# Attention on one core: two pairs of heads at a time, seven banks in rotation

## What is computed

```
x_norm = layernorm(xn, ln_g, ln_b)
q, k, v = x_norm @ Wq + bq, x_norm @ Wk + bk, x_norm @ Wv + bv      # (N, 8, 64)
ws  = (q[origin] . k[destination]) * SCALE * edge_weights           # per edge and head
att = softmax of ws over the edges of one origin
values = segment_sum(att * v[destination], origin)
y   = (values @ W1 + b1) @ W2 + b2
x   = x + (xn + y) + linear_attention(xn)                           # xn = layernorm(x), the layer's input
x   = x + ffn(layernorm(x))      # digits read out of 48 columns, shifted, added back as one-hot
```

## Time and profile before

| | us |
|---|---|
| median of 3 runs | 802.64 |
| lowest and highest | 800.6 and 811.86 |
| the profiled execution | 803.23 |
| its span in the trace | 801.5 |
| TensorE busy (PE) | 736.1 |
| VectorE busy (DVE) | 563.7 |
| ScalarE busy (ACT) | 388.2 |
| GpSimd busy (POOL) | 401.3 |
| attention's first scores | at 352.72 |

### The profile page before, as it was taken

The page is one execution under the profiler, slowest core; times in us unless marked ns, Lnnn a source line. Parts: engine busy times, 40 slices in busy tenths (PEclk is TensorE's granted clock), DMA queues, the critical chain, the costliest instruction groups (busy, mean ns, idle before and its releaser), DMA issues.

```text
span 801.5 us, 13739 instructions
## 1 busy us (share of the span) xinstructions
PE 736.1 (92%) x4643; PEld 446.3 (56%) x4682; DVE 563.7 (70%) x1295; ACT 388.2 (48%) x917; POOL 401.3 (50%) x399
## 2 busy tenths in 40 slices
PE   1997798898999999979999999999999999999984
PEld 0543345544445654436666666666666876667662
DVE  4468767684223252349998998999999887788696
ACT  0411110122130223117777777878788866566561
...
PEclk9999799998999999999999999999999999999996
...
GB/s 233 196 272 328 316 301 243 241 337 293 246 183 183 178 297 295 39 5 148 175 150 173 154 170 158 164 119 213 161 202 79 138 94 123 150 97 92 93 1 128
DMA packets 69636, 143.66 MB, mean 179 GB/s; under 512 B 22187, under 2 KB 54251, under 8 KB 65599
## 3 DMA queue, kind: packets, MB, share of 16 engines
...
...
## 4 chain that ended last, share of the span: by engine, by line
PE 76%; DVE 8%; SPq 6%; DMA 4%; ACT 3%; issue 2%; ACTq 1%; another core or an unknown queue 0%; DVEq 0%
PE bank L942 16%; PE bank L1176 12%; PE bank L1139 12%; PE bank L1158 11%; PE bank L936 9%; SPq L435 5%; PE bank L1204 4%; PE bank L1149 3%; DMA V<-in_edge_attr_dram 3%; PE bank L1182 2%; PE bank L1049 2%; DVE AR L1604 2%; PE bank L1000 1%; DMA kv_rows<-AR 1%; DVE lstat L1662 1%
## 5 line engine op out<-in xcount | busy, mean ns | idle before, releaser
L536 POOL DMA_INDIRECT w_tab<-pay,idx x330 | 340.6, 1032 | 154.5 <-issue 99.9
L1139 PE MATMUL bank<-KT,QT 64*128 64x512 f32 (+1 forms) x480 | 116.4, 562 | 4.4 <-DVE AR L1593 2.5
L1176 PE MATMUL bank<-AR,V 128*64 128x128 f32 (+1 forms) x1600 | 114.4, 281 | 0.0
L795 ACT ACTIVATE AR<-AR,nmx 128x512 f32<-128x512 f32 (+1 forms) x160 | 105.7, 662 | 14.4 <-DVE nmx L1608 14.4
L936 PE MATMUL bank<-AR 128*128 128x512 f32 (+1 forms) x288 | 106.1, 527 | 4.7 <-ACT QT L667 2.8
L942 PE MATMUL bank<-AR 128*128 128x512 f32 x240 | 108.1, 606 | 2.5 <-ACT AR L723 2.5
L1604 DVE CUSTOM_DVE_ANT_0 AR<-bank,AR,MX 128x512 f32<-128x512 f32 (+1 forms) x106 | 100.9, 990 | 9.3 <-remote 4.3
L609 POOL DMA_INDIRECT AR<-kv_rows,xd x10 | 10.6, 1063 | 179.3 <-PE bank L1176 159.2
L1176 PEld LDWEIGHTS bank<-AR,V 128*64 128x64 f32 (+1 forms) x1600 | 85.2, 137 | 20.6 <-issue 20.6
L803 ACT ACTIVATE bank<-AR 128x512 f32<-128x512 bf16 (+1 forms) x89 | 49.0, 551 | 78.0 <-DVE MX L1604 76.9
L936 PEld LDWEIGHTS bank<-AR 128*128 128x128 f32 x288 | 54.5, 192 | 51.6 <-issue 45.9
...
## 6 DMA issues: line engine op xcount, KB each, us to landing
...
```

The source lines that it names most:

```text
L536: pool.indirect_dma_start(out=w_tab, out_offset=bass.IndirectOffsetOnAxis(ap=idx[:, k, j:j + 1], axis=0), in_=pay[:, k % RING, j, :], in_o ...
L795: act.activation(ws[u % 3][hh][:, 0:n], ws[u % 3][hh][:, 0:n], ACT.Exp, bias=nmx[:, u % 4, hh:hh + 1], accum_out=DG[g][:, c, 2 * p + hh:2 ...
L1139: last = mm(bs[hh][:, 0:m], qs[hh], KT[64 * hh:64 * hh + 64, p, d0:d0 + m], start=not over, stop=over and g < 2, skip_group_check=over)
L1176: last = mm(bank[4 + w % 2][64 * hh:64 * hh + 64, p * P:(p + 1) * P], v, PT[u % 2][hh][0:rws, i * P:(i + 1) * P], start=(i == 0), stop=(i ...
```

## The change

The unit of the loops becomes a **step** `d` of two pairs; a round has an even step (q = 0, pairs 0 and 1) and an odd step (q = 1, pairs 2 and 3).

- TensorE does in step d: the scores of both pairs, then the masks that are not laid, then (inverse in even steps; factor, y and loser keys in odd steps), then the transposes of the last step's two pairs, then the values of the two pairs of the step before that. Inverse and y follow their round by two rounds now, not by one.
- A mask is laid by ScalarE for the second head of each second pair and for the first head of the odd step's first pair: three heads of a round, as before.
- Banks 0 to 6 go round among all products but values, in the order in which TensorE fills them (the list `USES`): `free` waits until the bank's previous use has been read, `gone` until this use has been read. Values have bank 7 alone.
- The odd copies (`odd_probs`, now in the middle of VectorE's step) go to ScalarE for one pair of four in group 1, where it was none, and three of four in groups 2 and 3, where it was two. `PT` has four pairs of buffers instead of two; the factor and some of them lie in the buffer of the edges' weights, which is free by then.
- VectorE waits head by head where it waited pair by pair, and `mask` for the next round stands between the last two products of the odd step.
- `bits(0)`, `digits(0)` and `finish(0)` stand behind the loop, after the last `scaled`; `added` of the last two tiles is there too.

```diff
--- before.py
+++ after.py
@@ -48,7 +48,8 @@
-SB = (0, 1, 6)
+ND = NU // 2
+NB = 7
 def on_act(u):
 
-    return u // 4 >= NT and u % 4 in (0, 1)
-def laid(u):
-
-    return u >= 2 and u % 4 != 0
+    return u % 4 in (0, 1, 2) if u // 4 >= NT else u % 4 == 1
+
+
+def laid(u, hh):
+
+    return (hh == 1 and u % 2 == 1 and u > 4) or (hh == 0 and u % 4 == 2 and u > 4)
...
+USES = []
+for _d in range(ND + 4):
+    _w, _q = _d // 2, _d % 2
+    if _d < ND:
+        USES += [("s",) + x for x in four(_d)]
+    if _q == 0 and 2 * NT <= _w - 2 < NW - 1:
+        USES += [("r", _w - 2)]
+    if _q == 1 and NT <= _w - 1 < NW:
+        USES += [("f", _w - 1)]
+    if _d == ND + 1:
+        USES += [("r", NW - 1)]
+    if _q == 1 and 2 * NT <= _w - 2 < NW:
+        USES += [("y", _w - 2)]
+    if _q == 1 and 2 * NT <= _w + 1 < NW:
+        USES += [("l", _w + 1)]
+    if 1 <= _d <= ND:
+        USES += [("t",) + x for x in four(_d - 1)]
+USE_OF = {what: i for i, what in enumerate(USES)}
...
+        def use(what):
+            return bank[USE_OF[what] % NB][:, :]
+        def free(eng, what):
+
+            r = USE_OF[what]
+            if r >= NB:
+                eng.wait_ge(s_bk[r % NB], r // NB)
+
+        def gone(eng, what):
+
+            r = USE_OF[what]
+            eng.wait_ge(s_bk[r % NB], r // NB + 1)
...
+            for d in range(ND + 1):
+                w, q = d // 2, d % 2
+                if q == 0 and 2 <= w <= NT + 1:
+                    keep(w - 2)
+                if q == 0 and NT <= w - 1 < NW:
                     change(w - 1)
+                if q == 0 and 2 * NT <= w - 2 < NW - 1:
+                    inverse(w - 2)
+                if q == 1 and 2 * NT <= w + 1 < NW:
+                    loser_k(w + 1)
+                if d >= 1:
+                    for u in (2 * d - 2, 2 * d - 1):
+                        probs(u, 0)
+                        if on_act(u):
+                            probs(u, 1)
+                if d < ND:
+                    exps(2 * d)
+                    if d + 1 < ND:
+                        for u, hh in four(d + 1):
+                            if laid(u, hh):
+                                lay_mask(u, hh)
+                    exps(2 * d + 1)
+            inverse(NW - 1)
+            root(0)
+            root(1)
+            normed()
...
+                for p in (2 * q, 2 * q + 1):
+                    u = 4 * w + p
+                    over = [laid(u, hh) for hh in range(2)]
+                    bs = [use(("s", u, hh)) for hh in range(2)]
+                    qs = [QT[64 * hh:64 * hh + 64, p, c * P:(c + 1) * P] for hh in range(2)]
+                    for hh in range(2):
+                        if over[hh]:
+                            pe.wait_ge(s_laid, LAID_OF[u, hh] + 1)
+                        else:
+                            free(pe, ("s", u, hh))
+                    for hh in range(2):
+                        last = mm(bs[hh][:, 0:m], qs[hh], KT[64 * hh:64 * hh + 64, p, d0:d0 + m], start=not over[hh], stop=over[hh] and g < 2, skip_group_check=over[hh])
...
+                for i, (u, hh) in enumerate(four(d)):
+                    if not laid(u, hh):
+                        mm(use(("s", u, hh))[:, 0:n], identb[:, :], pen[w % 2][:, 0:n], start=False, stop=True).then_inc(s_s[i], 1)
...
                     pe.wait_ge(s_exp, 2 * u + hh + 1)
-                    if u:
-                        pe.wait_ge((s_ea, s_ed)[hh], u)
-                    for i, (a, rws, _) in enumerate(blocks(g)):
+                    free(pe, ("t", u, hh))
...
-            for u in range(NU + 6):
+            for d in range(ND + 4):
+                w, q = d // 2, d % 2
+                if d < ND:
+                    scores(d)
+                if q == 0 and 2 * NT <= w - 2 < NW - 1:
+                    inverse(w - 2)
+                if q == 1 and NT <= w - 1 < NW:
                     factor(w - 1)
-                if p == 2 and 2 * NT < w <= NW:
-                    inverse(w - 1)
-                if p == 3 and 2 * NT < w <= NW:
-                    ffn(w - 1 - 2 * NT)
-                if p == 0 and 2 * NT - 1 <= w < NW - 1:
-                    loser_k(w + 1 - 2 * NT)
+                if d == ND + 1:
+                    values(NU - 2)
+                    values(NU - 1)
+                    inverse(NW - 1)
+                if q == 1 and 2 * NT <= w - 2 < NW:
+                    ffn(w - 2)
+                if q == 1 and 2 * NT <= w + 1 < NW:
+                    loser_k(w + 1)
+                if 1 <= d <= ND:
+                    transposes(d - 1)
+                if 2 <= d <= ND:
+                    values(2 * d - 4)
+                    values(2 * d - 3)
...
                 if u >= 3:
-                    dve.wait_ge(s_t, 2 * u - 4)
+                    dve.wait_ge(s_t, 2 * u - 5 + hh)
+                dve.wait_ge(s_s[2 * (u % 2) + hh], u // 2 + 1)
+                v.tensor_tensor_reduce(out=ws[u % 3][hh][:, 0:n], in0=use(("s", u, hh))[:, 0:n], in1=Wt[w % 2][:, 0:n, h],
...
-            for u in range(NU + 9):
+            for d in range(ND + 3):
+                w, q = d // 2, d % 2
+                if q == 0 and NT <= w - 1 < NW:
                     change(w - 1)
-                if p == 0 and 2 * NT + 1 < w <= NW + 1:
-                    added(w - 2 - 2 * NT)
-                if p == 2 and NT < w <= NW:
+                if q == 0 and NT <= w - 2 < NW:
+                    merged(w - 2)
+                if q == 0 and 2 * NT <= w - 2 < NW:
+                    scaled(w - 2)
+                if d < ND:
+                    weighted(2 * d, 0)
+                    weighted(2 * d, 1)
+                if 1 <= d <= ND:
+                    odd_probs(2 * d - 2)
+                if d < ND:
+                    shift_of(2 * d)
+                if q == 1 and NT <= w - 1 < NW:
                     rescaled(w - 1)
-                if p == 3 and NT < w <= NW:
-                    merged(w - 1)
-                if p == 3 and 2 * NT < w <= NW:
-                    scaled(w - 1 - 2 * NT)
-                if u < NU:
-                    weighted(u)
-                if 2 <= u <= NU + 1:
-                    odd_probs(u - 2)
-                if p == 1 and NT < w <= NW:
+                if d < ND:
+                    weighted(2 * d + 1, 0)
+                if q == 1 and w + 1 < NW:
+                    mask(w + 1)
+                if d < ND:
+                    weighted(2 * d + 1, 1)
+                if 1 <= d <= ND:
+                    odd_probs(2 * d - 1)
+                if d < ND:
+                    shift_of(2 * d + 1)
+                if q == 0 and NT <= w - 1 < NW:
                     denominators(w - 1)
-                if p == 2 and w < NW - 1:
-                    mask(w + 1)
-                if p == 3 and w == NW - 1:
-                    bits(0)
-                if p == 3 and w == NW:
-                    digits(0)
-                    finish(0)
-                if p == 2 and w == NW + 1:
-                    bits(1)
-                    digits(1)
-                if p == 0 and w == NW + 2:
-                    finish(1)
+                if q == 1 and 2 * NT <= w - 2 < NW - 2:
+                    added(w - 2)
+            bits(0)
+            added(NW - 2)
+            digits(0)
+            finish(0)
+            added(NW - 1)
+            bits(1)
+            digits(1)
+            finish(1)
```

245 lines of the change are left out of this document (102 added, 143 removed).

## The result

The changed kernel takes 840.51 us (median of 4 runs, 836.24 to 844.17), the kernel before 805.39 beside it: ratio 1.043, 95% interval 1.033 to 1.052. It is slower, by 35 us. The profiled execution took 840.8, its span is 839.1 against 801.5: 37.6 to explain.

A forecast was written before the change was run, and what follows sets the result against it. TensorE, busy 92% of the span, was taken to bound the kernel before. Terms +1.2 + 0 - 3.8 + 18.2 + 11.5 = +27.1 on the 801.5 span, plus 1.7 outside it, gave 830 us; range 790 to 842.

The forecast's parts named there:

- Column group 1, round 13.45: Chain of group 1: odd step waits for ScalarE's laid mask until 7.35; round 13.45 against 13.3, +1.2 for 9 rounds.
- Column group 2, round 13.9: Chain of group 2: even scores wait for the odd step's last product's bank; round 13.9 against 13.91, difference 0.
- a product frees its bank after 1.13, 354.21 to 355.34: VectorE's weighted product, used in the chain of group 1: its PSUM bank is released 1.13 us after it starts.
- they cost nothing: Tile loads by SyncE, issued a round ahead from the same point of VectorE's work: claimed to cost nothing.
- Column group 3, round 18.4: Chain of group 3: third product waits for transposes behind y; round 18.4 against 15.80, +18.2 over seven rounds.
- First two rounds of the group -3.8: Group 3's first two rounds, with neither inverse nor y: 12.5 and 11.5 against 27.83 together, -3.8.
- Last round and tail +11.5: Last round 18.0 and tail 33.7, bits and digits behind the last scaled: 51.7 against 40.24, +11.5.
- TensorE's own savings: Two pairs joined pay entry and exit once: scores 1.92, transposes 1.85, values 1.88; 0.9, 1.1, 1.75 us a round.
- Rival A: Whole kernel: TensorE stays the bound everywhere, waits fall on time spent anyway; -30.4, 773 us; chance 0.12.
- B: Group 3's chain breaks and 14.05 a round holds there, the rest as forecast; -10, 793 us; chance 0.13.
- C: Column groups 1 and 2 gain and group 3 loses; +6.8, 810 us; chance 0.10.
- Rival D: Holes in group 3's rounds bring half clock; y alone would double, 3.4 in each of 8 rounds; 857 us; chance 0.05.

The follow-up runs named there:

- the first experiment: In the changed kernel, ScalarE lays the masks of an odd step ahead of the even step's exponentials; 826.89 us, ratio to before 1.026.
- five edits: Changed kernel with odd steps' laid masks earlier, y behind transposes, early bits, scaled and rescaled rows behind products; 796.45 us, ratio to before 0.991.

## Why the prediction was right, and where it was off

The forecast was 830 (790 to 842), slower; the measurement is 840.5, inside the range by 1.5, and one of the four runs (844.2) lay outside it. In the spans 37.6 stand against 27.1 forecast. Of the 10.5 between them 6.6 are column group 2, more than twice what the prediction allowed for a chain of ten rounds (0.3 a round), 1.7 column group 1, 1.5 the start and 1.0 the end (group 3 gives back 0.3). So the direction and the chain that decides were right, and that the total stayed in the range is in part luck. By its own steps:

- *Column group 1, round 13.45.* Measured 13.49, the odd scores released by the laid mask 7.39 behind the even ones (7.35 forecast). Shown as the cause by the first experiment: with the mask laid sooner the round is 12.60. The 1.7 by which the ten rounds came out over the forecast sits in the second one, which took 15.19, mostly with the clock (below).
- *Column group 2, round 13.9: the mis-sized term.* Measured 14.45, in all 6.6 where 0 was forecast. The mechanism was right, each point of the chain late: odd scores 7.09 (6.85 forecast), first product 8.39 (8.12), third 11.53 (11.07), last one's bank free 14.44 (13.9). The step that was mis-sized is "a product frees its bank after 1.13, 354.21 to 355.34" and, with it, the 2.11 for two products and the shift: both were read in the first pair of column group 1. From column group 2 on the product starts from a stored maximum (MX among its inputs) and takes 1.13 to 1.16, where it took 1.07:

```profile
519.42 1.16 DVE L1649 CUSTOM_DVE_ANT_0 AR<-bank,AR,MX 128x512 f32<-128x512 f32 x1 [1.69 <-PE bank L1195]
...
520.50 1.15 DVE L1649 CUSTOM_DVE_ANT_0 AR<-bank,AR,MX 128x512 f32<-128x512 f32 x1
...
531.38 1.99 PE L1183 MATMUL bank<-KT,QT 64*128 64x512 f32 x8 [0.74 <-DVE MX L1649]
```

  The scores of this even step began at 516.93, its two products and the shift (at 521.77) take 2.35 and not 2.11, and the first product starts 2.49 behind the scores and not 2.35. Six products stand on the chain; at 0.08 each they are about 0.5 of the 0.54, an estimate. The other 1.2 of the 6.6 lies in rounds 11, 15 and 19 (14.91, 14.84 and 15.31), which were not worked apart. In round 15 VectorE waits 0.31 for the load of a tile at 573.39, and 1.5 and 1.9 at the same place in the runs with early bits and with five edits, so the prediction's "they cost nothing" for the tile loads does not hold in every round. Moving the rescaled row, a term that the chain named, took 0.54 off (0.55 to 0.69 expected).
- *Column group 3, round 18.4.* Measured 18.27, seven rounds 17.7 longer (18.2 forecast). First transpose 5.95 behind the scores (6.03), third product 6.48 (6.59), the inverse's turn 13.28 (13.48), scaled row 14.03 (14.26), products 14.64 and 15.37 (14.87, 15.62). The links were cut one at a time: y's place 0.88, the scaled row 1.20, the third product's buffer 1.42. Each alone is less than the 2.47 by which the round grew, and they do not add up: with the scaled row moved y's place is worth 0, behind five edits the buffer is worth 0.08, and the laid mask, worth 0 alone, is worth 0.42 behind the scaled row. It is a ring of waits, not a queue of costs.
- *First two rounds of the group -3.8*: measured -3.6. It is no saving: the rounds take 12.50 and 11.76 against 12.34 and 15.49 before, where the second already held an inverse and y. These now come a round later and are paid for at the end.
- *Last round and tail +11.5*: measured +12.5. The added(29)-to-end of 10.38 came back exactly (828.72 to 839.1). The early bits took 5.8 of the 12.5 away, so the bit work behind the last scaled row is about half of it. One more inverse and y than before fall there, 0.44 + 3.44 = 3.9 by the prediction's own terms, an estimate. Moving y took 3.0 off this part too (49.7). The granted clock hardly differs (0.82 against 0.84 before). How the rest divides was not tried.
- *TensorE's own savings.* Scores of two pairs measure 1.92 (441.59 to 443.51), transposes 1.84 (443.95 to 445.79), values 1.90 (445.79 to 447.69), forecast 1.92, 1.85 and 1.88. Rival A needed only that they be the time; the waits above refute it. B and C fell too: group 3 kept its chain, groups 1 and 2 lost.
- *Rival D, half clock.* Not in the seven rounds of group 3: their granted clock is 1.00 over 128 us with 22.8 us of holes. Ahead of them it came once, in the second round of all. In the run with the laid mask moved it did come in one round of group 3 (19.64 instead of 18.27), so what D describes does happen, at 1.4 for that round; as the state of every round it is refuted.
- *The start, +1.5.* Not a term of the prediction and, by the runs, none of the change: the first scores stand between 350.6 and 355.3 in nine profiles of kernels with the same code ahead of them.
